# Attention and expert layer: one-block units normed by VectorE before the transposition, moved steps, idle TensorE products

## The chip, the cores and the metric

The kernel runs on one core of a Trainium2 chip. A core has five engines with queues of their own: TensorE (PE: matrix products and transpositions, into PSUM; PEld is its weight load), VectorE (DVE), ScalarE (ACT), GpSimd (POOL) and SyncE (SP, which issues most transfers), and 16 DMA engines shared by all queues. TensorE's clock is granted at one of two levels, 1.2 or 2.4 GHz; a granted clock of 1.00 is the upper one, 0.50 the lower. The metric is the device time of one execution in microseconds (us), as the median of the runs.

## What is computed

```python
# B, T, M, D, G, H = 2, 1024, 256, 128, 4, 4; all float32
q = rope(einsum('bim,ghmd->bghid', x, w_aq)); k = rope(einsum('bim,gmd->bgid', x, w_ak))
v = einsum('bim,gmd->bgid', x, w_av)
s = einsum('bghid,bgjd->bghij', q * D**-0.25, k * D**-0.25) - 1e30 * (i < j)   # causal
o = einsum('bghij,bgjd->bghid', softmax(s), v)
x = layernorm(x + einsum('bghid,ghdm->bim', o, w_ao))
# router over E = 64 experts in 8 groups: the best 4 groups, then the best 6 experts of a token,
# weights = their sigmoid scores over their sum, times 2.5; at most 48 tokens an expert
y = sum over a token's experts of w * (silu(x @ w_gate) * (x @ w_up)) @ w_down
shared = silu(x @ ws_gate) * (x @ ws_up) @ ws_down
out = layernorm(x + y + shared)
```

## The kernel before

The 2048 tokens are 16 tiles of 128 (`TILES`), 8 to a batch. A unit u (64 of them, `UNITS`) is one tile and one of the 4 key groups: tile u // 4, group u % 4, with 4 query heads. Scores are causal, so the units of a batch's n-th tile need n blocks of 128 keys: `blocks(u)` (line 78) is 1 for units 0 to 3 and 32 to 35, 2 for 4 to 7 and 36 to 39, and 8 for the last tile of a batch.

There are four stages. Projections and rotary embedding come first (to about 150 us), with Q, K and V going through DRAM. Then the units (about 150 to 910). Then the tail of the last tile: its layer norm, router and choice of experts, and the scatter of its token rows into the experts' slots. Last come 32 pairs of experts, whose output rows are added in DRAM by indirect transfers of GpSimd's queue (`sums`, L922), and a final sum and layer norm.

Products at full precision are made in two ways: as fp32, or in three passes of operands that are split into a rounded high part (ScalarE, helper `split`, L938) and the rest (VectorE, helper `low`, L1341, or GpSimd: Q at L886, K of the second batch at L871, output weights at L876, the unit's output at L881).

For one unit the steps are:

- `score`: for each head, TensorE makes the row of scores in `s_ps` (L1193) and adds the causal mask (L1196); VectorE takes its negative maximum (`neg_max`, L1407);
- `exp`: ScalarE makes the exponentials in `probs` and their sum in `row_sum` (L1038);
- `ptrans`: for each block, TensorE transposes the four heads' block (L1203), and ScalarE copies it (`pt`, L1049; or `pt_hi`, L938, and VectorE `pt_lo`, L1341). At a unit's first block VectorE also takes the reciprocal of the sums (L1413) and transposes it in 32x32 squares to `inv_t` (L1414); SP stores it in four transfers to `inverses` (L768), waits until they have landed, and loads it back, the same row for all partitions, to `inv_row` (L772);
- `pv`: TensorE adds the block's product with V in `o_ps` (L1220 as fp32, L1223 as three passes); the output comes out transposed, with the queries along the free dimension, which is why the inverses are wanted as a row;
- `omul`: VectorE waits for `inv_row` and multiplies `o_ps` by it to `ot_raw` (L1425);
- `osplit`, `outproj`, `yadd`: the output's split, its product with the output weights (L1233 as fp32 for the first 12 units, L1242 after), and the sum over groups in `y_sb` (L1437).

Behind a tile's last `yadd` come `norm` (statistics L1441 to L1443, the power on GpSimd L895, the row L1449), `x1t` and `x1lo` (its transposition, L1251, and split), `rtr` (router and shared gate, L1258), `sig`, `shared` (L1463 to L1469), `ht`, `htlo`, `sd`, `zadd` (the shared expert: transposition L1264, product L1274, sum L1527), `pick` 0 to 7 (the choice, L1477 to L1511), `count` (L1268, L1269), `fit`, `place` (L1520 to L1535) and `scat` 0 to 2 (two of the six scatters of a row each, L909).

`schedule()` writes one sequence of steps, `SEQ`, and each engine runs through this same sequence and does its part of every step, in order; semaphores hold it where data isn't there. A head's slot in the sequence is one `score`, the `ptrans`, `pv` of an earlier unit (`late = H + 1` heads behind), one `exp`, and what the tables put there. `BETWEEN` (line 85) places the tile steps: each row has the step, how many tiles back it works, and at which of a tile's 16 heads it stands, one number each for the first, second, third and all further tiles of a batch. `KSPLIT_AT` and `WO_SPLIT_AT` (lines 151, 152) name the units in which a group of the second batch's K and of the output weights is split. `RINGED` steps share three PSUM banks in turn.

The queues in short: TensorE waits in `ptrans` for the unit's four exponentials only; VectorE, in its queue, waits before a unit's reciprocal until the stores of the unit two before have landed, and in `omul` for the load; SP waits in its queue for each landing. In the tail, TensorE waits for each result in turn and then for `attention_left`, which VectorE signals behind the last step (L1538); ScalarE waits until all scatters have landed and loads the slots (`srow`, L1077), for which the first expert's transposition on TensorE (L1287) waits.

## Time and profile before

| | |
|---|---|
| median of 3 runs | 1064.26 us (1063.52 to 1064.9) |
| the profiled execution | 1066.87 us, its span 1065.0 us |
| busy: TensorE, VectorE, ScalarE, GpSimd | 950.3, 710.2, 517.4, 447.2 us |
| mean granted clock | 0.958 |

The profile is of one execution. The page gives its totals, the span in 40 slices of 26.6 us, the chain that ended last (followed back from the last instruction, at each step to what released it) and the costliest groups. The trace behind it answers narrower questions: the instructions of an engine in order, with the idle time before each and what ended it, and the busy time in given stretches. Matmuls overlap, so their durations in a timeline are longer than the time they hold TensorE; the chain gives the latter. An fp32 product is recorded as two instructions. "Issue" is time in which the engine waited for nothing that the profile shows.

### The profile page before, as it was taken

The numbers are of one execution on the slowest core, as the hardware profiler recorded it, in microseconds if no ns is written. First come the engines' busy times: TensorE is split into PE (matmuls) and PEld (weight loads), VectorE is DVE, ScalarE is ACT, GpSimd is POOL, SyncE is SP. The second block draws the span as 40 slices with busy tenths as digits, with TensorE's granted clock in tenths as the row PEclk, the third lists the DMA queues.
The fourth block names the chain that finished last, engine by engine and source line by source line (L and its number), as shares of the span: only waits on it lengthen the run. The fifth ranks groups of instructions, "written<-read, shape, count | busy, mean of one in ns | idle before, by whom it ended". The sixth has DMA issues, their size and how long they took to land.

```text
span 1065.0 us, 17542 instructions
## 1 busy us (share of the span) xinstructions
PE 950.3 (89%) x5448; PEld 733.9 (69%) x5448; DVE 710.2 (67%) x1751; ACT 517.4 (49%) x1139; POOL 447.2 (42%) x390
## 2 busy tenths in 40 slices
PE   8999996979999999999968899999999999478744
PEld 6887875756788878777756667888778777245411
DVE  5989863757767676767657877677777676433326
ACT  4111133545656656565656556556566655134402
POOL 3878872244342414124257534424132231325711
PEclk9999998989999999999999999999999999679968
DMA  8786766422334211211234235321212033999687
GB/s 241 234 265 226 258 227 178 131 94 78 99 88 121 64 50 46 68 40 61 66 103 122 71 95 135 92 75 42 70 42 61 26 108 87 257 260 224 87 280 285
DMA packets 137306, 137.28 MB, mean 129 GB/s; under 512 B 18065, under 2 KB 108805, under 8 KB 137216
## 3 DMA queue, kind: packets, MB, share of 16 engines
q1 hardware_dynamic: 84064, 98.33, 30.0%
q10 hardware_dynamic: 43872, 29.50, 9.3%
...
q14 instruction: 45, 0.37, 0.1%
...
## 4 chain that ended last, share of the span: by engine, by line
PE 68%; DVE 9%; issue 7%; DMA 7%; POOL 3%; SPq 3%; ACT 2%; ACTq 1%; POOLq 0%; DVEq 0%
PE s_ps L1193 16%; PE ring L1203 10%; PE o_ps L1223 10%; PE o_ps L1220 7%; PE s_ps L1172 6%; PE ring L1242 6%; PE ring L1172 5%; DMA sums<-erow,goal_u 3%; SPq L811 2%; PE o_ps L1172 2%; DVE neg_max L1407 2%; PE ring L1233 2%; PE s_ps L1196 1%; POOL slot_rows L909 1%; DMA fsum<-sums 1%
## 5 line engine op out<-in xcount | busy, mean ns | idle before, releaser
L1038 ACT ACTIVATE probs<-s_ps,neg_max 128x128 f32<-128x128 f32 (+7 forms) x256 | 189.4, 740 | 118.8 <-DVE neg_max L1407 110.4
L1193 PE MATMUL s_ps<-kt,qt_hi 128*128 128x512 f32 (+3 forms) x768 | 230.9, 382 | 5.1 <-issue 2.4
L1407 DVE TENSOR_REDUCE neg_max<-s_ps 128x1 f32<-128x128 f32 (+7 forms) x256 | 191.5, 751 | 57.4 <-PE s_ps L1196 55.6
L1203 PE MATMUL ring<-ident,probs 128*128 128x128 f32 x1152 | 177.1, 277 | 19.1 <-ACT probs L1038 10.4
L1193 PEld LDWEIGHTS s_ps<-kt,qt_hi 128*128 128x128 f32 x768 | 137.4, 192 | 50.5 <-issue 29.4
L938 ACT ACTIVATE pt_hi<-ring 128x512 fp32r<-128x512 f32 x168 | 100.1, 596 | 141.1 <-PE ring L1203 138.6
L881 POOL TENSOR_TENSOR ot_lo<-ot_raw,ot_hi 128x512 fp32r<-128x512 f32 x52 | 66.7, 1283 | 240.1 <-ACT ot_hi L938 240.1
L1341 DVE TENSOR_TENSOR pt_lo<-ring,pt_hi 128x512 fp32r<-128x512 f32 x168 | 115.6, 689 | 67.9 <-ACT pt_hi L938 65.4
L1203 PEld LDWEIGHTS ring<-ident,probs 128*128 128x128 f32 x1152 | 128.8, 142 | 43.6 <-issue 24.3
L1223 PE MATMUL o_ps<-pt_hi,v 128*128 128x512 f32 x336 | 144.2, 430 | 0.0
L886 POOL TENSOR_TENSOR qt_lo<-q_raw,qt_hi 128x512 fp32r<-128x512 f32 x64 | 82.3, 1286 | 130.9 <-ACT qt_hi L938 130.5
L1193 PE MATMUL s_ps<-kt,qt_lo 128*128 128x512 f32 (+3 forms) x384 | 133.6, 348 | 0.0
L1220 PE MATMUL o_ps<-pt,v 128*128 128x512 f32 x240 | 125.1, 603 | 0.1
L866 POOL TENSOR_TENSOR prods<-prods 128x512 f32<-128x512 f32 x80 | 108.5, 1383 | 38.3 <-DVE prods L1394 38.0
L909 POOL DMA_INDIRECT slot_rows<-row,slot_u x96 | 94.9, 988 | 57.4 <-DVE slot_u L1535 36.0
L1049 ACT ACTIVATE pt<-ring 128x512 f32<-128x512 f32 x120 | 71.2, 593 | 50.0 <-PE ring L1203 49.8
L1425 DVE TENSOR_TENSOR ot_raw<-o_ps,inv_row 128x512 f32<-128x512 f32 x64 | 44.1, 689 | 58.7 <-PE o_ps L1223 33.3
L1193 PEld LDWEIGHTS s_ps<-kt,qt_lo 128*128 128x128 f32 x384 | 73.3, 191 | 8.2
L1223 PEld LDWEIGHTS o_ps<-pt_hi,v 128*128 128x128 f32 x336 | 63.8, 190 | 7.6 <-DVE pt_lo L1341 0.5
L1242 PE MATMUL ring<-wo,ot_hi 128*128 128x256 f32 x416 | 63.3, 295 | 5.9 <-ACT ot_hi L938 4.5
L1223 PE MATMUL o_ps<-pt_lo,v 128*128 128x512 f32 x168 | 66.3, 394 | 0.0
L922 POOL DMA_INDIRECT sums<-erow,goal_u x32 | 46.7, 1458 | 35.2 <-DVE dve_cell L1557 14.1
...
## 6 DMA issues: line engine op xcount, KB each, us to landing
...
q_raw<-qk_rows ACTq DMA_DIRECT2D x128, 128.0 KB, 2.9
...
```

The lines of the kernel that those rows point to most:

```text
L866: pool.tensor_tensor(pair[:, z, 0, :], pair[:, z, 0, :], pair[:, z, 1, :], op).then_inc(rot_ready, 1)
L909: pool.indirect_dma_start(slot_rows[:, :], bass.IndirectOffsetOnAxis(ap=slot_u[:, i % 2, k:k + 1], axis=0), row[:, i % 2, :], None, bounds ...
L938: return act.activation(hi, raw, ACT.Copy)
L1038: act.activation(probs[:, u % 2, h, 0:blocks(u) * P], s_ps[:, n % 2, score_cols(n)], ACT.Exp, bias=neg_max[:, n % 8:n % 8 + 1], accum_out= ...
L1172: ins = pe.matmul(bank(s), *sides, start=(turn == 0), stop=(turn == len(PROJ_PASSES) - 1))
L1193: pe.matmul(s_ps[:, n % 2, c + a:c + e], q[qp], k[kp][:, a:e], start=(qp == kp == 0), stop=(qp == 1 and not last))
L1203: ins = pe.transpose(bank(s)[:, h * P:(h + 1) * P], probs[:, u % 2, h, j * P:(j + 1) * P], ident[:, :])
L1220: ins = pe.matmul(o_ps[:, :], v_sb[i // NT][:, g, j, :], pt[:, n % PTB, :], start=first, stop=last)
L1223: ins = pe.matmul(o_ps[:, :], v[:, g, vp, j - VF, :], (pt_hi, pt_lo)[pp][:, n % PTB, :], start=False, stop=(last and vp == 1))
L1242: ins = pe.matmul(bank(s)[:, 0:M], (ot_hi, ot_lo)[op][:, h * P:(h + 1) * P], wo[:, g, wp, h, :], start=(op == wp == h == 0), stop=(op == 1 ...
L1341: return dve.tensor_tensor(lo, raw, hi.bitcast(F32), ALU.subtract)
L1407: dve.tensor_reduce(neg_max[:, n % 8:n % 8 + 1], s_ps[:, n % 2, score_cols(n)], AX_X, ALU.max, negate=True).then_inc(max_ready, 1)
```

## The change

1. Units of one block (`normed_first`: 0 to 3 and 32 to 35) no longer send their inverses through DRAM. At `ptrans`, behind the reciprocal, VectorE multiplies `probs` of all four heads by it in place (128x512, fp32) and signals `inv_ready`, for which TensorE's transposition now waits too. `omul` is a copy for them. SP's counts of these transfers go over the other units only (`normed_later`).
2. In `BETWEEN`, steps of a batch's second and third tile stand one head later: `ht`, `htlo`, `sd`, `zadd` of the tile two back, the first scatter in the third tile, `x1t` in both, `x1lo`, `rtr`, `sig` in the second, and in the third the next tile's `pick` 0, `ht`, `htlo`.
3. K's last group for the second batch is split one unit earlier (33 in place of 34), and its low part is made by VectorE and not by GpSimd. The output weights are split one head earlier in units 8 to 11.
4. TensorE makes fp32 products of the identity with itself, 128x128x128, into PSUM that nobody reads (`keep_at_work`): 8 ahead of the last tile's `x1t`, 10 ahead of its `ht`, 16 ahead of its `count`, 26 behind `attention_left`, then a wait until the last scatters have landed, then 8.

```diff
--- before.py
+++ after.py
@@ -84,13 +84,13 @@
 
 BETWEEN = [
     (("pick", 0), -2, (None, 0, 0, None)),
-    (("ht",), -2, (None, 1, 0, None)),
-    (("htlo",), -2, (None, 2, 1, None)),
+    (("ht",), -2, (None, 2, 1, None)),
+    (("htlo",), -2, (None, 3, 2, None)),
     (("pick", 1), -2, (None, 1, 1, None)),
     (("pick", 2), -2, (None, 2, 1, None)),
-    (("sd",), -2, (None, 3, 2, None)),
+    (("sd",), -2, (None, 4, 3, None)),
     (("pick", 3), -2, (None, 2, 2, None)),
-    (("zadd",), -2, (None, 4, 2, None)),
+    (("zadd",), -2, (None, 5, 3, None)),
     (("pick", 4), -2, (None, 3, 2, None)),
     (("pick", 5), -2, (None, 3, 2, None)),
     (("pick", 6), -2, (1, 4, 3, 0)),
@@ -98,21 +98,21 @@
     (("count",), -2, (2, 6, 5, 2)),
     (("fit",), -2, (2, 6, 5, 2)),
     (("place",), -2, (4, 7, 6, 4)),
-    (("scat", 0), -2, (5, 8, 7, 5)),
+    (("scat", 0), -2, (5, 8, 8, 5)),
     (("osplit",), -1, (6, 6, 6, 6)),
     (("outproj",), -1, (7, 7, 7, 7)),
     (("yadd",), -1, (8, 8, 7, 7)),
     (("scat", 1), -2, (9, 10, 9, 6)),
     (("norm",), -1, (9, 9, 8, 8)),
-    (("x1t",), -1, (11, 11, 9, 9)),
-    (("x1lo",), -1, (12, 12, 10, 9)),
+    (("x1t",), -1, (11, 12, 10, 9)),
+    (("x1lo",), -1, (12, 13, 10, 9)),
     (("scat", 2), -2, (13, 13, 13, 7)),
-    (("rtr",), -1, (13, 13, 11, 10)),
-    (("sig",), -1, (14, 14, 12, 10)),
+    (("rtr",), -1, (13, 14, 11, 10)),
+    (("sig",), -1, (14, 15, 12, 10)),
     (("shared",), -1, (15, 15, 12, 10)),
-    (("pick", 0), -1, (None, None, 13, 11)),
-    (("ht",), -1, (None, None, 13, 12)),
-    (("htlo",), -1, (None, None, 14, 12)),
+    (("pick", 0), -1, (None, None, 14, 11)),
+    (("ht",), -1, (None, None, 14, 12)),
+    (("htlo",), -1, (None, None, 15, 12)),
     (("pick", 1), -1, (None, None, 14, 13)),
     (("sd",), -1, (None, None, 15, 13)),
     (("zadd",), -1, (None, None, 15, 13)),
@@ -148,7 +148,7 @@
     return seq
 
 
-KSPLIT_AT = [NT * G - G + n for n in (1, 2, 3, 6)]
+KSPLIT_AT = [NT * G - G + n for n in (1, 2, 3, 5)]
 WO_SPLIT_AT = [8, 9, 10, 11]
 FIRST_ROUNDED = 3 * G
 WO_AT = [("exp", 1, 1), ("exp", 1, 3), ("exp", 2, 0), ("exp", 2, 2)]
@@ -156,6 +156,19 @@
 V_LOAD_AT = [(NT - 1) * G + n for n in (1, 2, 7, 8)]
 VSPLIT_AT = [NT * G + n for n in (2, 3, 5, 6)]
 BLANK_AT = [(c, name, 0, 1) for c in range(CHUNKS) for name in (0, 2)]
+
+
+NORMED_FIRST = 1
+
+
+def normed_first(u):
+
+    return blocks(u) <= NORMED_FIRST
+
+
+def normed_later(u):
+
+    return sum(not normed_first(n) for n in range(u))
 
 
 def schedule():
@@ -239,7 +252,7 @@
             drain(i * G)
         if h == 1 and u in KSPLIT_AT:
             seq.append(("ksplit", 1, KSPLIT_AT.index(u)))
-        if h == 3 and u in WO_SPLIT_AT:
+        if h == 2 and u in WO_SPLIT_AT:
             seq.append(("wosplit", WO_SPLIT_AT.index(u)))
         misc(i, n % (G * H))
     p = TILES - 1
@@ -760,14 +773,14 @@
                         load_x(TILES + s[1] + XB)
                     for i in range(s[1] + 1 if s[1] else 0, min(s[1] + 2, TILES)):
                         blank_sums(i)
-                if s[0] == "ptrans" and s[2] == 0:
-                    u = s[1]
+                if s[0] == "ptrans" and s[2] == 0 and not normed_first(s[1]):
+                    u, n = s[1], normed_later(s[1])
                     sp.wait_ge(inv_ready, u + 1)
-                    used(sp, inv_loaded[u % 2], 16 * (u // 2))
+                    used(sp, inv_loaded[u % 2], 16 * (n // 2))
                     for a in range(P // 32):
                         sp.dma_start(inverses[u % 2, :].rearrange("(h a q) -> a h q", h=H, q=32)[a, :, :],
                                      inv_t[32 * a:32 * a + H, u % 2, :]).then_inc(inv_stored, 16)
-                    sp.wait_ge(inv_stored, 64 * (u + 1))
+                    sp.wait_ge(inv_stored, 64 * (n + 1))
                     used(sp, o_ready, u - 1)
                     sp.dma_start(inv_row[:, u % 2, :],
                                  inverses[u % 2:u % 2 + 1, :].to_broadcast([P, P * H])
@@ -865,7 +878,7 @@
                     for z, op in enumerate((ALU.subtract, ALU.add)):
                         pool.tensor_tensor(pair[:, z, 0, :], pair[:, z, 0, :], pair[:, z, 1, :], op
                                            ).then_inc(rot_ready, 1)
-                if s[0] == "ksplit" and s[1] == 1:
+                if s[0] == "ksplit" and s[1] == 1 and s[2] < G - 1:
                     b, g = s[1:]
                     pool.wait_ge(k_hi_ready, G * b + g + 1)
                     pool.tensor_tensor(kt_lo[:, g, :], k_source(b, g), kt_hi[:, g, :].bitcast(F32),
@@ -1133,6 +1146,11 @@
                 elif r >= PRE_BANKS:
                     pe.wait_ge(ring_read[r - RING], PRE_TURNS[r - RING])
 
+            def keep_at_work(n):
+
+                for _ in range(n):
+                    pe.matmul(s_ps[:, 0, 0:P], ident[:, :], ident[:, :], start=True, stop=True)
+
             pe.wait_ge(ident_ready, 1)
             for s in SEQ:
                 kind = s[0]
@@ -1199,6 +1217,8 @@
                 if kind == "ptrans":
                     u, j = s[1:]
                     pe.wait_ge(probs_ready, H * (u + 1))
+                    if normed_first(u):
+                        pe.wait_ge(inv_ready, u + 1)
                     for h in range(H):
                         ins = pe.transpose(bank(s)[:, h * P:(h + 1) * P], probs[:, u % 2, h, j * P:(j + 1) * P],
                                            ident[:, :])
@@ -1245,6 +1265,8 @@
                     ins.then_inc(attn_ready, 1)
                 if kind == "x1t":
                     i = s[1]
+                    if i == TILES - 1:
+                        keep_at_work(8)
                     pe.wait_ge(x1_ready, i + 1)
                     xc = row[:, i % 2, 0:M].rearrange("t (p c) -> t c p", c=MC)
                     for c in range(MC):
@@ -1260,10 +1282,14 @@
                                             start=(c == 0 and xp == wp == 0), stop=(c == MC - 1 and xp == 1))
                     ins.then_inc(rtr_ready, 1)
                 if kind == "ht":
+                    if s[1] == TILES - 1:
+                        keep_at_work(10)
                     read(pe, ("rtr", s[1]))
                     pe.transpose(bank(s)[0:F, 0:P], hid[:, :], ident[:, :]).then_inc(ht_ready, 1)
                 if kind == "count":
 
+                    if s[1] == TILES - 1:
+                        keep_at_work(16)
                     pe.wait_ge(chose_ready, s[1] + 1)
                     pe.matmul(bank(s)[:, 0:E], before_bf[:, :], chose[:, :], start=True, stop=False)
                     pe.matmul(bank(s)[:, 0:E], ones_bf[:, :], taken[:, :], start=False, stop=True
@@ -1277,6 +1303,9 @@
 
 
             pe.wait_ge(attention_left, 1)
+            keep_at_work(26)
+            pe.wait_ge(scattered[(TILES - 1) % 2], 8 * K * TILES)
+            keep_at_work(8)
 
             def slots_t(n):
                 if n in CHUNK_AT:
@@ -1396,6 +1425,10 @@
                     g = s[2]
                     dve.wait_ge(k_hi_ready, g + 1)
                     low(kt_lo[:, g, :], k_source(0, g), kt_hi[:, g, :]).then_inc(k_ready, 1)
+                if s == ("ksplit", 1, G - 1):
+                    dve.wait_ge(k_hi_ready, B * G)
+                    dve.wait_ge(k_ready, B * G - 1)
+                    low(kt_lo[:, G - 1, :], k_source(1, G - 1), kt_hi[:, G - 1, :]).then_inc(k_ready, 1)
                 if kind == "projv" and VF <= s[1] < NT:
                     j = s[1] - VF
                     dve.wait_ge(v_hi_ready, j + 1)
@@ -1409,9 +1442,14 @@
                 if kind == "ptrans" and s[2] == 0:
                     u = s[1]
                     dve.wait_ge(probs_ready, H * (u + 1))
-                    used(dve, inv_stored, 64 * (u - 1))
+                    used(dve, inv_stored, 64 * (normed_later(u) - 1))
                     after(dve.reciprocal(inv_sum[:, u % 2, 0:H], row_sum[:, u % 2, :]))
-                    dve.transpose(inv_t[:, u % 2, :], inv_sum[:, u % 2, :]).then_inc(inv_ready, 1)
+                    if normed_first(u):
+                        raw = probs[:, u % 2, :, 0:blocks(u) * P]
+                        dve.tensor_tensor(raw, raw, each(inv_sum[:, u % 2, 0:H], blocks(u) * P), ALU.mult
+                                          ).then_inc(inv_ready, 1)
+                    else:
+                        dve.transpose(inv_t[:, u % 2, :], inv_sum[:, u % 2, :]).then_inc(inv_ready, 1)
                 if kind == "ptrans" and s[2] >= VF:
                     n = PT_AT[s[1:]]
                     dve.wait_ge(p_hi_ready, PS_AT[s[1:]] + 1)
@@ -1419,10 +1457,14 @@
                 if kind == "omul":
                     u = s[1]
                     i, g = divmod(u, G)
-                    dve.wait_ge(inv_loaded[u % 2], 16 * (u // 2 + 1))
                     dve.wait_ge(pv_done, PT_AT[(u, blocks(u) - 1)] + 1)
                     used(dve, attn_ready, u - 1)
-                    dve.tensor_tensor(ot_raw[:, u % 2, :], o_ps[:, :], inv_row[:, u % 2, :], ALU.mult).then_inc(o_ready, 1)
+                    if normed_first(u):
+                        dve.tensor_copy(ot_raw[:, u % 2, :], o_ps[:, :]).then_inc(o_ready, 1)
+                    else:
+                        dve.wait_ge(inv_loaded[u % 2], 16 * (normed_later(u) // 2 + 1))
+                        dve.tensor_tensor(ot_raw[:, u % 2, :], o_ps[:, :], inv_row[:, u % 2, :], ALU.mult
+                                          ).then_inc(o_ready, 1)
                 if kind == "yadd":
                     u, s = s[1], ("outproj", s[1])
                     i, g = divmod(u, G)
```

## Rows read from the trace of the kernel before

**Rows 1.** The page: clock by slice, and chain that ended last, by engine.
```profile
PEclk9999998989999999999999999999999999679968
...
PE 68%; DVE 9%; issue 7%; DMA 7%; POOL 3%; SPq 3%; ACT 2%; ACTq 1%; POOLq 0%; DVEq 0%
```

**Rows 2.** Stretches (us): busy time (instructions) of PE, PEld, DVE, ACT, POOL; granted clock; DMA share.
```profile
164.70:173.20 8.50, 0.00 (x0) 0.00 (x0) 2.22 (x8) 0.92 (x5) 0.00 (x0) 0.75 0.70 198
...
173.20:179.30 6.10, 6.07 (x23) 4.69 (x24) 2.28 (x6) 3.56 (x11) 1.26 (x1) 0.51 0.39 125
...
228.00:234.00 6.00, 5.97 (x22) 5.04 (x23) 3.03 (x8) 2.20 (x7) 1.91 (x2) 0.51 0.37 126
```

**Rows 3.** Chain that ended last, in order of time (start, us, what).
```profile
160.23 5.83 DMA inverses<-inv_t
...
166.07 5.26 DMA inv_row<-inverses
...
179.84 1.73 PE ring L1233 x8
...
234.78 0.71 PE ring L1258 x6
```

**Rows 4.** TensorE's timeline: start, us, instruction [idle before, what ended it].
```profile
173.23 1.09 PE L1203 MATMUL ring<-ident,probs 128*128 128x128 f32 x4 [8.56 <-ACT probs L1038]
...
201.88 0.29 PE L1264 MATMUL ring<-ident,hid 128*96 128x128 f32 x1 [1.58 <-DVE hid L1469]
...
228.03 0.67 PE L1251 MATMUL ring<-ident,row 128*128 128x128 f32 x2 [4.19 <-DVE row L1449]
...
240.49 0.28 PE L1264 MATMUL ring<-ident,hid 128*96 128x128 f32 x1 [2.44 <-DVE hid L1469]
...
546.90 0.41 PE L1193 MATMUL s_ps<-kt,qt_hi 128*128 128x128 f32 x2 [2.44 <-issue]
...
558.67 0.36 PE L1274 MATMUL ring<-wsd_hi,ht_hi 96*128 96x256 f32 x1 [2.41 <-DVE ht_lo L1341]
...
618.87 0.28 PE L1264 MATMUL ring<-ident,hid 128*96 128x128 f32 x1 [1.69 <-DVE hid L1469]
```

**Rows 5.** Groups of VectorE by form: busy us, mean ns.
```profile
L1604 DVE TENSOR_TENSOR fsum<-fsum 128x512 f32<-128x512 f32 x20 | 13.8, 690 | 31.2 <-DMA fsum<-sums 30.8
...
L1341 DVE TENSOR_TENSOR kt<-kt 128x1024 fp32r<-128x1024 f32 x4 | 4.9, 1229 | 0.0
```

**Rows 6.** Timelines of VectorE and GpSimd, one collision.
```profile
586.70 2.26 DVE L1477 TENSOR_TENSOR biased<-sig,bias_sb 128x64 f32<-128x64 f32 x1
...
587.58 1.30 POOL L886 TENSOR_TENSOR qt_lo<-q_raw,qt_hi 128x512 fp32r<-128x512 f32 x1
```

**Rows 7.** GpSimd's timeline behind the second tile.
```profile
220.93 2.37 POOL L876 TENSOR_TENSOR wo<-wo_raw,wo 128x1024 fp32r<-128x1024 f32 x1 [7.02 <-ACT wo L938]
...
225.90 0.59 POOL L895 TENSOR_TENSOR rstd<-var_eps,minus_half 128x1 f32<-128x1 f32 x1
```

**Rows 8.** ScalarE's and VectorE's timelines at unit 32.
```profile
534.79 0.60 ACT L1049 ACTIVATE pt<-ring 128x512 f32<-128x512 f32 x1 [0.49 <-PE ring L1203]
...
535.83 0.17 DVE L1413 RECIPROCAL inv_sum<-row_sum 128x4 f32<-128x4 f32 x1
...
536.64 0.69 DVE L1425 TENSOR_TENSOR ot_raw<-o_ps,inv_row 128x512 f32<-128x512 f32 x1 [0.22 <-issue]
```

**Rows 9.** Chain that ended last, in the tail.
```profile
917.94 1.64 PE ring L1258 x6
...
920.80 0.24 DVE biased L1477
...
923.47 0.19 DVE chose L1502
...
941.88 1.49 PE s_ps L1297 x8
...
947.32 0.81 PE s_ps L1297 x8
```

## The prediction

> **What bounds the kernel now.** I read the page first. The chain that ended last lies on TensorE for 68% of the span, with VectorE, DMA and "issue" far behind, and the granted clock is full in nearly all slices except around the seventh, the ninth and tenth, and the last five [rows 1]. So the middle of the kernel is TensorE work at full speed that nothing in the change touches, and a gain has to come from places where TensorE stands still or runs at 1.2 GHz. I then cut the span into stretches and read TensorE's timeline for what ends each pause. There are three such places: the start of each batch (units 0 to 11 and 32 to 43, where score rows are 1 to 3 blocks long), and the tail behind the last unit.
>
> The largest pause is at the start: TensorE does nothing at all from 164.70 to 173.20 and works the next 6.1 us at half clock [rows 2]. Its row says "waits for ScalarE's exponentials" [rows 4], but the chain shows the root: four stores of the inverse sums, 5.83 us to land, then their broadcast load, 5.26 us [rows 3]. VectorE stands in its queue behind the first (the reciprocal of unit 2 waits until unit 0's stores have landed) and then behind the second (the product with unit 0's inverses), so the row maxima of unit 3 come late, then its exponentials, then TensorE.
>
> **A. Units 0 to 3 normed before the transposition.** For these the change removes four stores, one load, and both waits of VectorE. It adds one in-place product of 128x512, both inputs in SBUF, for which the nearest row is the addition of two such tiles, 690 ns [rows 5]. The 32x32 transposition goes (about 0.2 us, not counted), and the output product becomes a copy of the same 128x512 out of PSUM; I take that as no cheaper. The new wait is TensorE's: the transposition of a unit now waits for reciprocal and product, 0.17 [rows 8] + 0.69 = 0.9 us behind the last exponential. Behind it on TensorE are the next scores, and behind those the next row maxima. Written out unit by unit, each of units 0 to 3 gets some 0.7 us longer (0.9 less what the Q split's wait hides), so the fourth transposition comes at 167.8, an estimate, in place of 173.23 [rows 4]; the clock then had no idle stretch to fall in, so the 6.0 us of unit 4 that ran at half clock become about 3.6 us, where ScalarE's exponentials set the pace. Unit 4's transposition comes at 171.4 in place of 179.2: **gain 7.8 us**. From there to 190 TensorE has no pause before, so the shift stays. What is late next: the output weights, loaded by GpSimd's queue just before the pause and used by the first output product, which moves from 179.84 [rows 3] to 172; and the Q tiles. The DMA engines are still at 0.70 in the pause [rows 2]. Bounds: 5 us (both late by 1.5 us, and each product held up) to 9 us.
>
> **B. Steps of tiles 1 and 2 set apart, output-weight split one head earlier.** Three pauses: 1.58, 4.19 and 2.44 us [rows 4]. The 4.19 one is a queue on GpSimd: it splits output weights for 2.37 us, issues two row scatters, and only then raises the variance to -0.5 (at 225.90) [rows 7], for which VectorE's normalisation and TensorE's transposition of x1 wait. The scatter moves one head back, behind the power, and the transposition one head back too, so I expect this pause to go; the same holds for 1.58 and 2.44, whose transposition of the hidden tile gets one more head (1.2 us or more of TensorE work) ahead of it. That is 8.2 us at most; I count 6.0, as the split, one head earlier, now holds GpSimd while VectorE ranks the experts (a collision, below). The 6 us from 228 on ran at half clock [rows 2]; without the pause they take some 3.5. I count 2.0. **Gain 8.0 us**, bounds 3 and 11.
>
> **C. Units 32 to 35, and the last K split.** The split of K's last group goes from GpSimd (2.34 us and a pause of 2.44 us on TensorE [rows 4]) to VectorE, one unit earlier: 1.23 us [rows 5]. Gain 2.4. The hidden tile's step moves: 2.41 us [rows 4], of which I count 1.4; 1.2 for a half-clock spell at 548. Against that: here no wait on the inverses is to be seen, so the normed product brings nothing and costs its wait. Unit 32's transposition was through by 534.8, but VectorE came to its reciprocal at 535.83 only, behind the ranking of tile 6 [rows 8]. TensorE will now stand from before 534.8 until 536.9 (535.83 + 0.9, and a hand-over), then VectorE waits for ScalarE's K copy and splits K before it evacuates unit 31, so that this comes at about 540 in place of 536.64 [rows 8]: -3.5. The other three units cost 0.5 each. **Net 0**, bounds -4 and +3.
>
> **D. Tiles 8 to 10.** The same pauses as in B without the weight split, 1.69 us the largest [rows 4], about 5 us in all. VectorE is nearly full here. **Gain 2.0**, bounds 0 and 4.
>
> **E. The tail.** An idle product is an fp32 128x128x128; eight fp32 instructions of 256 columns, four products, took 1.73 us [rows 3], so 0.22 us each at full clock and 0.43 at half. The first eight start at half clock and end some 0.6 us after the row they should have ended before: -0.6. Then the router's six products, 1.64 us here and 0.71 at full clock [rows 9, 3], and two transpositions: +1.3. The sixteen ahead of the count have from about 919 to 923.5, when the choice is written [rows 9], and need 3.5 us at full clock. The ten and the 26 lie under VectorE's and the scatters' time. If the clock is then high when the first experts start, their group of eight takes 0.81 in place of 1.49 us [rows 9], and the first output row comes 2.4 us earlier; since the scatters behind it stand under weight loads until 975, I count 1.3 of it. **Gain 2.0**, bounds -2 and 4.
>
> **A new wait.** Where pauses are this close, closing one shows another; for the pauses of 0.3 to 0.7 us that appear at new places I take off **2.0**.
>
> **Sum.** 7.8 + 8.0 + 0 + 2.0 + 2.0 - 2.0 = 17.8 us. The profiled execution took 1066.87 us (span 1065.0), so it would come to 1049.1; the median of the runs is 2.6 us lower, 1064.26, and the forecast for it is 1064.26 - 17.8 = **1046.5 us**.
>
> **A rule that speaks against it.** VectorE's addition of the bias, two inputs in SBUF, took 2.26 us beside GpSimd's splits (one ended at 587.6, the next started at once) and 0.24 us where GpSimd was quiet [rows 6, 9]. The Trainium skill says the same (SBUF — State Buffer, "SBUF: two separate sides"): VectorE and GpSimd share a port pair, and whichever of a GpSimd operation and a two-input VectorE operation starts first has it to its end. So the new product can be held up by a Q split of 1.30 us [rows 6]. In my unit-by-unit order it starts 0.3 us before the Q split, and the split waits instead; so the sum holds nothing for it.
>
> **The rivals.**
> (1) The early gain is eaten by loads: Q tiles or output weights are late, so TensorE meets a DMA wait in place of the inverses'. The DMA engines' share of 0.70 in the pause [rows 2] speaks for it, that nothing waited for these loads before says little. A gives 3 in place of 7.8, and half of the clock's part of B goes: 1052.5.
> (2) The moved steps only shift the pauses, because VectorE is the limit there: B gives 3, D 0: 1053.5.
> (3) Slower: each of the eight normed products finds GpSimd at a Q split and waits for it. Then a transposition is late by 0.9 + 1.3 = 2.2 us in eight units, 17.6 us; that is 10.8 over the 0.7 x 4 + 0.5 x 8 counted, and with pauses like the 4.19 us one, behind which the clock fell, it falls again (A and B lose 5, E 2) and C's queue doubles (-3.5): 17.8 - 10.8 - 7 - 3.5 = -3.5, so 1067.8. It decides as soon as the product starts behind the split in most units.
> (4) The change does not do what it says, the clock stays at half through the tail and the idle products run over: E is -2: 1050.5. This lies in the forecast's own range.
>
> **Chances.** Forecast with (4): 0.60; (1) 0.14; (2) 0.17; (3) 0.06; rest 0.03 for a loss or standstill by something not seen. The forecast's range is 1040 to 1051; taking in (1) and (2), and the upper bounds of A and B on the other side, 1039 to 1056. A difference of under 0.2%, 2.1 us, can't be told from none: faster 0.92, same 0.03, slower 0.05.
>
> **What would show it.** Right: no pause of over 2 us on TensorE between 150 and 250, and no half-clock stretch behind 164; unit 4's transposition near 171; a TensorE wait of 0.7 to 1 us on VectorE's new product in units 0 to 3; the x1 transposition of tile 1 without a pause; a TensorE pause of 2 to 3 us near unit 32's transposition; the clock at full for the last router and for the first experts. Wrong: pauses ended by DMA behind unit 3; VectorE products of over 1.5 us at the new line; the sixteen idle products still running when the choice is written.

## The result, and the profile after

The changed kernel took 1072.46 us (median of 20 runs, 1062.71 to 1077.33), the kernel before 1062.99 us beside it (20 runs, 1056.99 to 1066.07): ratio 1.0084, 95% interval 1.0066 to 1.0102. It is 0.8% slower, 8.9 us by the ratio, where 1046.5 us and a gain were forecast, with a range of 1040 to 1051. The profiled execution took 1068.99 us, so the two profiles are only 2.1 us apart where the medians are 9.5 apart. Both profiles are off their medians, in opposite directions: that of before is long at its start, that of after short behind unit 63 (table below). Stretches are therefore read over all profiles, not from these two alone.

Clock by slice and the chain that ended last, on the page of the changed kernel (answers to [rows 1]):
```profile
PEclk9999988999999999999969999999999999999968
...
PE 72%; DVE 10%; issue 5%; DMA 5%; SPq 2%; ACT 2%; POOL 1%; ACTq 1%; POOLq 0%; DVEq 0%
```
The dip of the ninth slice is gone, the one at the sixth and seventh (units 0 to 5) is wider; a new one, deeper than both, stands in slice 21, at units 33 to 36, and the tail keeps its clock better.

TensorE's pauses in the changed kernel (start, us, instruction, in brackets the idle time before it and what ended it; answers to [rows 4]):
```profile
152.46 0.66 PE L1223 MATMUL ring<-ident,probs 128*128 128x128 f32 x4 [1.63 <-DVE probs L1449]
157.93 1.09 PE L1223 MATMUL ring<-ident,probs 128*128 128x128 f32 x4 [1.82 <-DVE probs L1449]
163.83 1.08 PE L1223 MATMUL ring<-ident,probs 128*128 128x128 f32 x4 [1.83 <-DVE probs L1449]
...
198.31 1.99 PE L1253 MATMUL ring<-wo_raw,ot_raw 128*128 128x256 f32 x8 [1.02 <-DVE hid L1511]
...
231.16 3.55 PE L1253 MATMUL ring<-wo_raw,ot_raw 128*128 128x256 f32 x8 [1.81 <-DVE hid L1511]
...
240.25 0.36 PE L1300 MATMUL ring<-wsd_hi,ht_hi 96*128 96x256 f32 x1 [2.70 <-DVE ht_lo L1370]
...
530.08 0.63 PE L1223 MATMUL ring<-ident,probs 128*128 128x128 f32 x4 [2.55 <-DVE probs L1449]
535.50 2.05 PE L1262 MATMUL ring<-wo,ot_hi 128*128 128x256 f32 x8 [2.65 <-ACT ot_hi L951]
541.61 0.69 PE L1223 MATMUL ring<-ident,probs 128*128 128x128 f32 x4 [2.27 <-DVE probs L1449]
547.39 1.09 PE L1223 MATMUL ring<-ident,probs 128*128 128x128 f32 x4 [1.78 <-DVE probs L1449]
557.73 1.08 PE L1223 MATMUL ring<-ident,probs 128*128 128x128 f32 x4 [4.09 <-DVE probs L1449]
```
The pause of 8.56 us has become one in each unit, ended by the new product (L1449). In the L1223 rows the second column is the same four transpositions at two speeds: about 0.63 us at full clock, 1.09 at half. Two of the three early ones shown run at half. The clock fell behind the first of these pauses: it was granted at 1.00 from 144.40 to 152.46 and at 0.54 from there to the next transposition.

Why a unit takes so long, in VectorE's timeline for unit 2 of the changed kernel:
```profile
160.49 0.29 DVE L1440 TENSOR_REDUCE neg_max<-s_ps 128x1 f32<-128x128 f32 x1 [0.48 <-PE s_ps L1214]
161.27 0.29 DVE L1440 TENSOR_REDUCE neg_max<-s_ps 128x1 f32<-128x128 f32 x1 [0.48 <-PE s_ps L1214]
162.04 0.29 DVE L1440 TENSOR_REDUCE neg_max<-s_ps 128x1 f32<-128x128 f32 x1 [0.48 <-PE s_ps L1214]
162.25 0.17 DVE L1446 RECIPROCAL inv_sum<-row_sum 128x4 f32<-128x4 f32 x1
162.45 1.24 DVE L1449 TENSOR_TENSOR probs<-probs,inv_sum 128x512 f32<-128x512 f32 x1
```
The maxima come every 0.77 us, each behind TensorE's score (in e8, the filled kernel below, TensorE needs 0.41 for one). The reciprocal stands behind the one at 162.04, which belongs to head 1 of the *next* unit. The product then takes 1.24 us, not 0.69. TensorE's transposition waits for all of it, and the next scores wait behind that. Not every product is held up like this one. The other seven took 1.04, 1.23 and 0.69 us in units 0, 1 and 3, and 0.69, 0.69, 1.19 and 0.69 us in units 32 to 35. Three of the eight (units 1, 2 and 34) began while GpSimd was at a Q split; the one of unit 0 began while it was at another operation, a product of the rotary embedding. The ones of units 34 and 35:
```profile
546.06 1.19 DVE L1449 TENSOR_TENSOR probs<-probs,inv_sum 128x512 f32<-128x512 f32 x1
556.89 0.69 DVE L1449 TENSOR_TENSOR probs<-probs,inv_sum 128x512 f32<-128x512 f32 x1
```

Stretches of the two kernels (us from:to, length; busy time and instructions of PE, PEld, DVE, ACT, POOL; granted clock; DMA share and GB/s). In the kernel before, units 0 to 4, and 32 to 45:
```profile
147.32:178.23 30.91, 20.87 (x120) 17.19 (x120) 11.23 (x34) 12.44 (x48) 12.87 (x12) 0.80 0.62 191
518.68:644.07 125.39, 106.71 (x674) 82.91 (x673) 90.36 (x271) 72.52 (x192) 67.60 (x57) 0.99 0.33 94
```
The same two in the changed kernel, with the worst part of the first between them:
```profile
144.40:174.10 29.70, 23.00 (x120) 19.36 (x120) 14.38 (x34) 13.12 (x47) 13.84 (x12) 0.71 0.58 176
150.00:168.00 18.00, 12.71 (x69) 11.21 (x68) 8.12 (x21) 8.83 (x32) 9.21 (x9) 0.62 0.73 212
511.96:650.16 138.20, 114.40 (x674) 88.98 (x674) 92.65 (x272) 72.33 (x192) 65.79 (x56) 0.91 0.27 77
```
Units 32 to 45 take 12.8 us more. TensorE's instructions are the same 674 in number, but it is busy 7.7 us longer with them (clock 0.91 in place of 0.99) and stands 5.1 us longer. The early stretch has lost its long pause and yet is hardly shorter.

All 16 experiments and the changed kernel, as ratio to the kernel before with its 95% interval, and the length of four stretches of each profile, in us. A stretch goes from the first score of head 0 of one unit (the product of its causal mask, L1214 after) to that of the other; the last one goes to the end of the span.

| kernel | ratio | units 0 to 5 | 5 to 20 | 32 to 46 | 63 to end |
|---|---|---|---|---|---|
| before | | 30.9 | 158.4 | 125.4 | 188.5 |
| changed | 1.0084 (1.0066–1.0102) | 29.7 | 155.8 | 138.2 | 184.7 |
| e1 no unit normed | 0.9990 (0.9966–1.0015) | 29.5 | 156.9 | 128.1 | 187.2 |
| e2 norm alone | 1.0113 (1.0079–1.0148) | 32.1 | 157.5 | 138.4 | 187.6 |
| e3 units 0–3 only | 0.9986 (0.9961–1.0011) | 30.7 | 156.5 | 127.8 | 186.8 |
| e4 no idle products | 1.0099 (1.0069–1.0130) | 30.5 | 156.4 | 135.5 | 189.3 |
| e5 old steps | 1.0062 (1.0025–1.0098) | 32.3 | 157.0 | 134.3 | 187.1 |
| e8 filled | 1.0024 (0.9997–1.0052) | 22.5 | 157.2 | 134.9 | 186.2 |
| e9 by head | 1.0138 (1.0105–1.0170) | 35.1 | 157.0 | 138.6 | 189.6 |
| e10 early | 1.0034 (1.0008–1.0060) | 24.6 | 155.9 | 134.7 | 185.5 |
| e11 idle products alone | 0.9995 (0.9969–1.0022) | 29.6 | 156.8 | 125.8 | 190.1 |
| e12 first four | 0.9891 (0.9851–0.9932) | 21.8 | 155.2 | 125.2 | 188.4 |
| e13 + K on VectorE | 0.9915 (0.9888–0.9942) | 21.8 | 155.4 | 123.3 | 189.4 |
| e14 filled and early | 0.9984 (0.9961–1.0008) | 23.7 | 156.0 | 134.3 | 189.8 |
| e15 steps alone | 1.0018 (0.9997–1.0039) | 29.2 | 157.1 | 128.8 | 187.5 |
| e16 steps filled | 0.9970 (0.9952–0.9989) | 31.4 | 157.4 | 124.9 | 185.5 |
| e17 gap filled | 0.9951 (0.9927–0.9975) | 26.5 | 155.8 | 125.8 | 187.1 |
| e18 + one pause filled | 0.9899 (0.9865–0.9934) | 21.9 | 155.5 | 125.0 | 188.6 |

Each ratio is against the kernel before as it ran beside that experiment; one execution of e12 (1374.95 us) and one of the kernel before (1234.96 us) ran in a slower state and are left out. Each stretch is from one profile. Kernels that differ in nothing inside a stretch show how far one profile can be off: units 32 to 46 took 138.2 us in the changed kernel and 135.5 in e4, 123.3 in e13 and 125.0 in e18, 128.1 in e1 and 127.8 in e3; units 0 to 5 took 30.9 in the kernel before and 29.6 in e11. Where a stretch and the ratios differ, the ratios over all runs decide.

### The profile page after: what moved, and what is told of

The parts are those of the page before. It is cut to its first block, busy times and chain, and to the rows that moved or that the text cites. A ratio compares the mean times of both kernels' runs of the same rounds, so it can differ in the third digit from the quotient of the medians.

```text
span 1067.2 us, 17751 instructions
## 1 busy us (share of the span) xinstructions
PE 972.3 (91%) x5584; PEld 755.1 (71%) x5584; DVE 717.1 (67%) x1752; ACT 516.8 (48%) x1139; POOL 446.6 (42%) x389
## 4 chain that ended last, share of the span: by engine, by line
PE 72%; DVE 10%; issue 5%; DMA 5%; SPq 2%; ACT 2%; POOL 1%; ACTq 1%; POOLq 0%; DVEq 0%
PE s_ps L1211 17%; PE ring L1223 11%; PE o_ps L1243 10%; PE o_ps L1240 8%; PE ring L1262 6%; PE s_ps L1190 6%; PE ring L1190 5%; DMA sums<-erow,goal_u 3%; SPq L824 2%; PE ring L1253 2%; DVE neg_max L1440 2%; PE o_ps L1190 2%; PE s_ps L1214 1%; DMA fsum<-sums 1%; PE ring L1280 1%
## 5 line engine op out<-in xcount | busy, mean ns | idle before, releaser
L1051 ACT ACTIVATE probs<-s_ps,neg_max 128x128 f32<-128x128 f32 (+7 forms) x256 | 189.3, 740 | 114.4 <-DVE neg_max L1440 105.2
L1211 PE MATMUL s_ps<-kt,qt_hi 128*128 128x512 f32 (+3 forms) x768 | 237.3, 391 | 1.5 <-DVE prods L1423 1.5
L1223 PE MATMUL ring<-ident,probs 128*128 128x128 f32 x1152 | 178.0, 278 | 24.9 <-DVE probs L1449 17.4
L1211 PEld LDWEIGHTS s_ps<-kt,qt_hi 128*128 128x128 f32 x768 | 141.3, 198 | 50.9 <-issue 31.6
L1223 PEld LDWEIGHTS ring<-ident,probs 128*128 128x128 f32 x1152 | 129.3, 143 | 49.7 <-issue 33.3
L1240 PE MATMUL o_ps<-pt,v 128*128 128x512 f32 x240 | 128.2, 617 | 0.2
L922 POOL DMA_INDIRECT slot_rows<-row,slot_u x96 | 95.6, 996 | 57.2 <-issue 32.3
L1466 DVE TENSOR_TENSOR ot_raw<-o_ps,inv_row 128x512 f32<-128x512 f32 x56 | 38.5, 688 | 42.0 <-PE o_ps L1243 37.4
L1262 PEld LDWEIGHTS ring<-wo,ot_hi 128*128 128x128 f32 x416 | 54.3, 192 | 15.3 <-issue 7.3
```

The costliest lines, as they stand in the source:

```text
L922: pool.indirect_dma_start(slot_rows[:, :], bass.IndirectOffsetOnAxis(ap=slot_u[:, i % 2, k:k + 1], axis=0), row[:, i % 2, :], None, bounds ...
L1051: act.activation(probs[:, u % 2, h, 0:blocks(u) * P], s_ps[:, n % 2, score_cols(n)], ACT.Exp, bias=neg_max[:, n % 8:n % 8 + 1], accum_out= ...
L1211: pe.matmul(s_ps[:, n % 2, c + a:c + e], q[qp], k[kp][:, a:e], start=(qp == kp == 0), stop=(qp == 1 and not last))
L1223: ins = pe.transpose(bank(s)[:, h * P:(h + 1) * P], probs[:, u % 2, h, j * P:(j + 1) * P], ident[:, :])
L1240: ins = pe.matmul(o_ps[:, :], v_sb[i // NT][:, g, j, :], pt[:, n % PTB, :], start=first, stop=last)
L1262: ins = pe.matmul(bank(s)[:, 0:M], (ot_hi, ot_lo)[op][:, h * P:(h + 1) * P], wo[:, g, wp, h, :], start=(op == wp == h == 0), stop=(op == 1 ...
```

## The experiments

### Which part of the change costs the time

e1, no unit normed:
```diff
-NORMED_FIRST = 1
+NORMED_FIRST = 0
```


> The changed kernel with no unit normed ahead of its transposition; moved steps, the K split on VectorE and the idle products stay. Theory N (the normed product is what made the change slower: in the profiles, units 32 to 45 lose 12.9 us, and TensorE's pauses there, 2.55, 2.65, 2.27, 1.78 and 4.09 us, are mostly ended by the normed product or what is queued behind it): the loss of 12.9 goes and the 8.5 us pause at unit 2 comes back, so about 8 to 12 us less than the kernel before, ratio 0.989 to 0.993. Theory S (the moved steps and the K split on VectorE caused the loss of 32 to 45): it stays slower than before, 1.003 to 1.010.


e3, `return u < 4` in `normed_first`:


> The changed kernel with units 0 to 3 alone normed; units 32 to 35 go by the stored inverses again. Theory N: the loss of units 32 to 45 goes, the early part stays at its gain of 6.7 us up to unit 20, the tail gives its 4: 9 to 13 us less than before, ratio 0.988 to 0.992, within 3 us of the kernel without any normed unit. Theory S: the loss in units 32 to 45 stays, ratio 1.003 to 1.010.


e2, the kernel before with the norm for the eight units and nothing else:


> The kernel before with units 0 to 3 and 32 to 35 normed ahead of the transposition, and nothing else of the change. Theory N: slower than before by 9 to 14 us (1.008 to 1.013), with units 32 to 45 losing some 12 us and units 0 to 3 gaining next to nothing. Theory S: within 3 us of the kernel before, as the product costs only its own 0.7 us or so each, and unit 2's pause is saved. My forecast's own terms for it would have been a gain of about 3 (7.8 less 3.5 and 1.5).


Measured: 0.9990, 0.9986 and 1.0113. The norm alone makes the kernel slower by 12 us (8 to 16), at least as much as the whole change's 9 (7 to 11), and the loss of units 32 to 46 goes with units 32 to 35 (138.2 to 128.1 or 127.8). The ratios say so by themselves: e3 differs from the changed kernel in units 32 to 35 alone and is 0.0098 below it, 10.4 us (7 to 14). Theory N holds for the place and the size of the loss. Its further claim, that 8 to 12 us of gain would then come out, fails: without the norm the rest of the change is worth about 1 us (e1's interval goes from 3.6 us faster to 1.6 slower). Nor do units 0 to 3 gain by their norm: e3 has it and e1 does not, and they are 0.4 us apart. Something is left in units 32 to 46 all the same, as the stretch of e1 shows (TensorE's busy time is the number behind the length):
```profile
513.81:641.87 128.06, 110.05 (x675) 85.96 (x674) 90.80 (x272) 72.19 (x192) 66.21 (x56) 0.96 0.33 92
```
That is 2.7 us over the kernel before, all of it in busy time (110.05 against 106.71) at a clock of 0.96: it is taken up below.

e4, no idle products in the tail (`for _ in range(0 * n)` in `keep_at_work`), and e11, the kernel before with them alone:


> The changed kernel without the idle products in the tail. If they give the 4 us that the profiles show behind unit 63 (clock at full for the last router and the first experts), it is 3 to 5 us slower than the changed kernel: ratio to the kernel before 1.011 to 1.014. If the sixteen products that overrun the choice eat the clock's gain, it is the same as the changed kernel or 1 us faster, 1.007 to 1.009.

> The kernel before with the idle products of the tail alone; no other part of the change. My forecast's term for them was 2.0 us, bounds -2 and 4. In six profiles with them the stretch behind unit 63 was 1.8 us shorter on the mean than in the kernel before, in two without them 0.1 shorter. Expected if that holds: 1 to 3 us less, ratio 0.997 to 0.999. If the sixteen that overrun the choice eat it up: 0.999 to 1.001.


Measured 1.0099 and 0.9995, against 1.0084 and 1: a gain of 1.6 and of 0.5 us, neither distinct from none. The 1.8 us that e11 was to confirm came from too few profiles. The stretch behind unit 63 took 187.6 us on the mean of 13 profiles with the products and 188.0 on that of 5 without, and scatters by 5 us. In the changed kernel the clock is high there (the router's six products take 0.95 us in place of 1.64), but the sixteen overrun. Two pieces of the chain that ended last in the changed kernel (start, us, what), the router and then the sixteen:
```profile
923.41 0.95 PE ring L1280 x6
924.36 5.20 PE s_ps L1152 x32
```
And the step of VectorE's timeline, same kernel, that they were to end ahead of, the choice:
```profile
928.28 0.20 DVE L1544 TENSOR_SCALAR chose<-left 128x64 bf16<-128x64 f32 x1
```
The choice is there at 928.48, the sixteen products (32 instructions) end at 929.56: 1.1 us late, partly at half clock. So these take back at least a part of what the clock gives; no run has the other idle products without the sixteen.

e5, old places of the steps and of the output weights' split, all else as changed; e15, the kernel before with only the new places:


> The changed kernel with the old places of the steps between the heads and of the output weight split; normed units, K split on VectorE and idle products stay. My forecast counted 10 us for them (8.0 at tiles 1 and 2, 2.0 at tiles 8 to 10) and 1.4 of the hidden tile's: then this kernel is 8 to 11 us slower than the changed one, ratio 1.016 to 1.019. If the steps only move the pauses (in the profiles the five pauses of 0.6 to 2.7 us between 198 and 241 add up to 7.1 us where three made 8.2 before): within 3 us of the changed kernel, ratio 1.006 to 1.011.

> The kernel before with the moved steps and the output weight split one head earlier, and nothing else of the change. My forecast's terms for it were 8.0 (tiles 1 and 2), 2.0 (tiles 8 to 10) and 1.4: 11 us less, ratio 0.990. If the steps only move the pauses, 0 to 2 us less, 0.998 to 1.000. If, as the kernel without normed units suggests (units 32 to 46 took 128.1 us in place of 125.4, with 3.3 us more of TensorE's work time and no more pause), the new pauses of over 3 us let the clock fall: 0 to 4 us more, 1.000 to 1.004.


Measured 1.0062 and 1.0018. Against the changed kernel the old places are 2.3 us faster and against the kernel before the new ones 1.9 us slower, neither clear of noise; a gain of 10 us is excluded. The pauses only moved. Of the three between 200 and 241 in the kernel before, 1.58, 4.19 and 2.44 us [rows 4], the 4.19 us one is indeed gone. In the changed kernel there are 1.02 and 0.61 us near 200 instead, then 0.92, 1.81 and 2.70 us between 224 and 241, 7.1 us in place of 8.2; in e1, e8, e10 and e15 the last of them is 4.3 us. VectorE is late with `hid` and `ht_lo` once the other step no longer holds TensorE.

### Why the normed product costs so much

Three edits to the changed kernel, each on one suspected cause. e8 puts TensorE to work ahead of its wait (theory G, clock):
```diff
+FILL = 6
...
                 if kind == "ptrans":
                     u, j = s[1:]
+                    if normed_first(u):
+                        for _ in range(FILL):
+                            pe.matmul(bank(s)[:, 0:P], ident[:, :], ident[:, :], start=True, stop=True)
                     pe.wait_ge(probs_ready, H * (u + 1))
```


> The changed kernel with six more idle products ahead of the first transposition of each normed unit, written into the PSUM bank that the transposition then overwrites. Theory G (the 1.4 to 1.8 us that TensorE stands for the normed product in each unit keep its clock at half, and the half clock lengthens the scores of the loop, 0.77 in place of 0.46 us a head): with TensorE at work the clock stays at full, a unit takes 4 to 4.5 us in place of 5.9 to 6.8, units 0 to 3 gain 4 us or more and 32 to 35 about as much, ratio to the kernel before 0.999 to 1.003. Theory P (the length of the product beside GpSimd's Q split, 1.04 to 1.24 in place of 0.69 us, and its place in the queue set the pace, the clock does not): no gain, ratio 1.007 to 1.011.


e9 writes the product as four of one input each (theory P, port):
```diff
-                        dve.tensor_tensor(raw, raw, each(inv_sum[:, u % 2, 0:H], blocks(u) * P), ALU.mult
-                                          ).then_inc(inv_ready, 1)
+                        for h in range(H):
+                            ins = dve.tensor_scalar(raw[:, h, :], raw[:, h, :], inv_sum[:, u % 2, h:h + 1], None,
+                                                    ALU.mult)
+                        ins.then_inc(inv_ready, 1)
```


> The changed kernel with the product written as four products of 128x128 by one column each, a form with one tile as input in place of two. Theory P (two tiles read from SBUF by VectorE collide with GpSimd's split): the four together take the same 0.7 to 0.9 us beside a split as alone, the split is no longer stretched to 1.8 us, the pauses get 0.4 us shorter, 2 to 4 us less than the changed kernel, ratio 1.005 to 1.007. Theory G alone: the product's length is a third of the pause at most, ratio 1.007 to 1.010.


e10 moves reciprocal and product ahead of the row maximum of the next unit's head 1 (theory Q, queue). Beside the lines shown, the block that takes the row maximum (`if kind == "score"`) moves behind this one:
```diff
-                if kind == "ptrans" and s[2] == 0:
-                    u = s[1]
+                if (kind == "ptrans" and s[2] == 0 and not normed_first(s[1])
+                        or kind == "score" and s[2] == 1 and s[1] >= 1 and normed_first(s[1] - 1)):
+                    u = s[1] if kind == "ptrans" else s[1] - 1
```


> The changed kernel with reciprocal and product one step earlier in VectorE's order, ahead of the row maximum of head 1 of the next unit (in the changed kernel they stand behind it, and it waits for its score on TensorE). Theory Q (the place in VectorE's queue is what makes TensorE wait): the product starts 0.7 to 0.9 us earlier in each of the eight units, pauses of 1.4 to 1.8 us become 0.6 to 0.9 us; 4 to 8 us less than the changed kernel, ratio 1.001 to 1.005. Theory G or P without Q: the maximum now waits for the product in its turn, so the score loop is as long as before, ratio 1.007 to 1.010.


e8 came to 1.0024, 6.4 us less than the changed kernel, and e10 to 1.0034, 5.3 us less (each give or take 3.5). So the clock and the place in the queue both count. By the table most of that lies in units 0 to 5, 7.2 and 5.1 us; in units 32 to 46 the two are at 134.9 and 134.7 us, under the changed kernel's 138.2 but hardly under e4's 135.5. Units 0 to 4 in e8:
```profile
146.19:168.67 22.48, 22.20 (x168) 19.83 (x168) 13.07 (x34) 12.39 (x46) 14.58 (x12) 1.00 0.76 227
```
48 instructions more than in the changed kernel and 7.2 us less, at a clock of 1.00 in place of 0.71. TensorE is busy for all but 0.3 us. The faster scores also let the product start before GpSimd's split in units 1 to 3, so that it took 0.69 us (timeline of e8, unit 1):
```profile
157.00 0.69 DVE L1453 TENSOR_TENSOR probs<-probs,inv_sum 128x512 f32<-128x512 f32 x1
157.17 1.65 POOL L900 TENSOR_TENSOR qt_lo<-q_raw,qt_hi 128x512 fp32r<-128x512 f32 x1
```
In e10 the pauses of units 1 and 2 fell from 1.82 and 1.83 to 0.51 us each, at a clock of 0.79 over the stretch. The shorter pauses alone did not bring the clock back. Behind the 1.64 us of unit 0 it fell, and the transpositions of units 1 and 2 still ran at half (TensorE's timeline in e10):
```profile
157.37 0.63 PE L1223 MATMUL ring<-ident,probs 128*128 128x128 f32 x4 [1.64 <-DVE probs L1444]
160.96 1.09 PE L1223 MATMUL ring<-ident,probs 128*128 128x128 f32 x4 [0.51 <-DVE probs L1444]
165.54 1.09 PE L1223 MATMUL ring<-ident,probs 128*128 128x128 f32 x4 [0.51 <-DVE probs L1444]
```

e9 went the other way, 1.0138. Its four small products took 0.87 us where GpSimd was quiet and up to 2.18 beside GpSimd's work (VectorE's timeline in e9, units 0, 1 and 32):
```profile
153.90 2.18 DVE L1450 TENSOR_SCALAR probs<-probs,inv_sum 128x128 f32<-128x128 f32 x4
...
160.20 1.50 DVE L1450 TENSOR_SCALAR probs<-probs,inv_sum 128x128 f32<-128x128 f32 x4
...
536.92 0.87 DVE L1450 TENSOR_SCALAR probs<-probs,inv_sum 128x128 f32<-128x128 f32 x4
```
So one input in place of two is no way around the collision here. P's assumption of the form is refuted; that the collision costs is not. How much it costs can be bounded: over the eight products of the changed kernel, what each took beyond 0.69 us adds up to 1.9 us (2.9 in the profiles of e2 and e4), of a loss of 9. In unit 1 of the changed kernel the split ran from 155.98 to 157.24 and the product, begun at 156.55, ended 0.54 us after it; with the order turned, in e8 above, it is the split that grows, from 1.26 to 1.65. The Trainium skill has the rule (SBUF — State Buffer, "SBUF: two separate sides": the one that starts first has the shared ports for the whole instruction, the other is blocked). By it the product would take the rest of the split, 0.69, and its own 0.69, 1.38 us; the trace has 1.23, so it agrees but for 0.15 us.

e14, both cures (six idle products and the earlier place) in all eight units:


> The changed kernel, all eight units normed, with both cures at once: product one step earlier and six idle products ahead of each normed transposition. Each alone gave 5 to 6 us. If they act on the same pause (the clock for one, its length for the other), together they give 7 to 10 of the 9 us lost, ratio 0.998 to 1.001; if the idle products now take longer than the pause they fill, 1.001 to 1.004. Above 0.999 it is behind the version that norms units 0 to 3 alone, since units 32 to 35 wait for no inverses.


Measured 0.9984. The early part keeps its gain, but units 32 to 46 are still at 134.3 us, 6.2 over e1. There the product replaces no wait. VectorE comes to it late from other steps, and 24 idle products have to be paid: against e1, TensorE is busy 5.6 us longer (115.65 against 110.05) and stands 0.6 longer. No cure made the norm pay in units 32 to 35.

### The clock by itself

e17, the kernel before with 32 idle products ahead of unit 3's transposition, in the 8.56 us pause:
```diff
+FILLED = {("ptrans", 3, 0): 32}
...
+                for _ in range(FILLED.get(s, 0)):
+                    pe.matmul(bank(s)[:, 0:P], ident[:, :], ident[:, :], start=True, stop=True)
```


> The kernel before, its pause of 8.6 us ahead of unit 3's transposition filled with 32 idle products (7.0 us at full clock), and nothing else. It measures the clock's part of that pause by itself: unit 4's scores and the transpositions behind the pause ran 6 us at half clock in the kernel before. If the clock is kept by any work of TensorE, units 0 to 5 take 27 us in place of 29.6, ratio 0.997 to 0.999; if it falls all the same, 29.6 us, 0.999 to 1.001.


Units 0 to 4 of e17, the same stretch as above:
```profile
145.74:172.28 26.54, 24.14 (x184) 21.56 (x184) 10.27 (x32) 11.84 (x45) 12.90 (x12) 1.00 0.70 215
```
0.9951, 5.2 us gained without touching the wait for the inverses, and the clock is 1.00 throughout. The interval is 2.6 to 7.8 us. In the profile the stretch is 3.0 us shorter than in e11, whose instructions up to there are the same but for the filling, and units 5 to 20 are 0.9 shorter.

e16, e1 with 12 and 11 idle products in the two 3.3 us pauses that the new step places leave in units 32 to 37 (`FILLED = {("outproj", 31): 12, ("sd", 7): 11}`, with the same loop):


> The kernel without normed units, its two pauses of 3.3 us in units 32 to 37 (ahead of an output product, ahead of the shared experts' product of tile 7) filled with 12 and 11 idle products. If half clock behind these pauses is the 3 us that the moved steps cost there, units 32 to 46 go from 128.1 to about 125 us and no slice there is under full clock; ratio 0.995 to 0.998. If the pauses themselves are the cost, nothing moves, 128 us, 0.998 to 1.001.


Units 32 to 45 of e16:
```profile
517.61:642.48 124.87, 111.99 (x721) 87.87 (x720) 90.70 (x272) 72.24 (x192) 66.34 (x56) 0.99 0.33 94
```
Clock 0.99 in place of 0.96, 124.9 in place of 128.1 us, ratio 0.9970 in place of 0.9990. So the 3 us that the moved steps cost there are the clock behind longer pauses, as expected; this rests on the stretch, as the two ratios' intervals overlap. The idle products themselves took 0.24 us each (24 instructions, 2.90 us, ahead of the output product).

### A version that beats both

e12: old steps, old K split, idle products of the tail, units 0 to 3 normed with the earlier place and four idle products each. e13: the same with K's last group on VectorE.


> Old steps, old K split, the idle products of the tail, and units 0 to 3 normed with both cures at once: reciprocal and product ahead of head 1's row maximum, and four idle products in front of each normed transposition. By the trace of the filled kernel, which gained 8.4 us between units 0 and 5, and by 1.8 us in the tail: 7 to 10 us less than the kernel before, ratio 0.990 to 0.993. If the two cures do not add and idle products now stand in the transposition's way (four are 0.9 us at full clock, the pause left was 0.5 at half): 3 to 6 us less, 0.994 to 0.997.

> The same as the kernel of the first four units, but K's last group of batch 2 is split by VectorE one unit earlier, as in the changed kernel. My forecast counted a gain of 2.4 us for it: then 2 to 3 us less than without it. If VectorE is what TensorE waits for in units 32 to 37, its 1.2 us there are added in part: 0 to 2 us more than without it.


Units 0 to 4 of e12:
```profile
147.92:169.76 21.84, 20.64 (x152) 18.06 (x152) 13.28 (x34) 12.37 (x46) 13.92 (x12) 1.00 0.79 238
```
0.9891 and 0.9915: 9 to 12 us less than the kernel before and, with e18 below, the fastest measured. The early stretch is 7.8 us shorter than in e11, the same number as term A's. Some 3 us of it e17 has too, by filling the old pause and without any norm. The K split takes 1.9 us off units 32 to 46 between these two profiles, but e18, with the same split, is at 125.0, 0.2 under e12; the forecast of 2.4 is neither confirmed nor excluded, and the ratios can't tell the two kernels apart.

e18: e13 with 16 idle products ahead of the transposition of tile 1's rows:


> The version with units 0 to 3 normed and K's last split on VectorE, with 16 idle products in the pause of 4.2 us ahead of the transposition of tile 1's rows. The clock stood at half for some 5 us behind that pause: 1 to 3 us less than without them, units 5 to 20 in 153.5 us in place of 155.4, ratio 0.987 to 0.991. If the pause has its own length from VectorE and GpSimd and the clock falls later all the same: as without them, 0.991.


0.9899: 1.7 us under e13 and 0.9 over e12, neither a difference that can be told. The pause of 4.20 us shrank to 0.53 and TensorE reached the hidden tile's step some 1.6 us earlier; there the wait for `hid` was as long as before (2.44 against 2.43), the clock fell behind that pause instead (0.70 from 225 to 230), and the stretch stayed at 155.5 us. My expectation of 153.5 us for this stretch failed; the ratio lies in the span that I expected, and the gain of 1 to 3 us is neither shown nor excluded by it.

## Why the prediction was wrong

**A, forecast +7.8, measured about -1.** The mean of units 0 to 5 is 30.1 us over the five profiles that norm nothing and fill nothing there, e16 among them, and 31.1 over the five with the changed kernel's norm. The ratios of e3 and e1, with and without this norm, are 0.4 us apart. Three statements of the step failed. (1) "0.17 + 0.69 = 0.9 us behind the last exponential": the reciprocal also stands behind the maximum of the next unit's head 1. (2) "the product starts 0.3 us before the Q split": in units 1 and 2 of the kernel as built it started 0.57 us behind it and took 1.23 and 1.24 us. (3) "the clock then had no idle stretch to fall in": the pauses of 1.6 to 1.8 us in every unit were enough here, and the mean clock from 150 to 168 was 0.62. I had written waits of 0.7 to 0.9 us a unit into the sum and never asked what they do to the clock. With TensorE kept at work and the product one step earlier, two edits that the forecast did not have, the early stretch does come out 7.8 us shorter (e12); that it is the very number forecast is partly luck.

**B and D, forecast +8.0 and +2.0, measured about +1 and -3.** Rival 2's mechanism: the steps only shift pauses. Between units 5 and 20 the means are 157.4 (old places, first batch otherwise uncured: before, e2, e5, e11) and 156.6 us (ten kernels with the new ones). That 0.8 us is not a gain of the places for certain: with the first batch cured, e12, e13, e17 and e18 have the old places and took 155.2 to 155.8 us, e8, e10 and e14 the new ones and 155.9 to 157.2. In units 32 to 46, e15 is 3.0 us longer than e11, e5 3.9 shorter than the changed kernel (1.2 shorter than e4). "I expect this pause to go" came true for the 4.19 us one. The failed step is what follows it, "the same holds for 1.58 and 2.44": in their place stand 1.02, 0.61, 1.81 and 2.70 us (4.3 for the last in e1, e8, e10 and e15). It looked at the step released and not at the next one in VectorE's queue. For D the term also left out the clock behind the new pauses of 3.3 us (e16).

**C, forecast 0, measured about -8 for its own two parts (-5.5 if e4's profile stands for the changed kernel).** The mechanism was as told ("TensorE will now stand from before 534.8"), the K split's 2.4 measured 1.9 in one pair of profiles and 0.2 in another, and the first pause of 2.55 us came as forecast. Mis-sized was "the other three units cost 0.5 each": their pauses are 2.27, 1.78 and 4.09 us. Against e1, with the same steps, the changed kernel is 10.1 us longer there (e4 7.4, the ratios of e3 and the changed kernel 10.4): TensorE stands 5.8 us longer (23.80 against 18.01) and is busy 4.35 us longer (114.40 against 110.05) at lower clock. The last pause lies behind steps of the ranking, one of them 0.94 us beside GpSimd.

**E, forecast +2.0, measured about +0.4, not distinct from none.** The clock is high, as forecast. The overrun of the sixteen was given as a sign of "wrong", and it is there.

**The sum.** Norm early -1.0, steps +0.8 and -3.0, norm late -10.1, K split +1.9, tail +0.4: -11.0 us, against -8.9 (-7.0 to -10.8) by the ratio. Single profiles of the same stretch differ by up to 2.7 us, so this is as close as it gets, and the agreement of the parts is no proof of each.

**The rivals.** Rival 3, given 0.06, is the nearest: normed products held up at GpSimd's split, pauses, and a clock that falls for them; it named 1067.8. Its direction and its clock are right, its main price is not. It charged each of eight products 1.3 us for a split; three of the eight began behind one (four in e2 and e4), and all collisions together lengthened the products by 1.9 us (2.9 there), where it added 10.8 us to the forecast's sum. Nor was its own condition, behind the split in most units, met over the eight. What it had too small is the rest, the clock and VectorE's queue. Its sum also has a slip: it takes off 0.5 us for eight units where the forecast had counted it for three besides unit 32; with four it would have named 1069.8. A reading was off too, without consequence: the clock's second dip is at the ninth slice alone, not at the tenth.

The order that rival 3 has, the product behind the split, was the one that I had ruled out by writing the units out at full clock. That order was itself a result of the clock: with TensorE kept at work (e8) the product does start before the split in units 1 to 3, as it does with the earlier place (e10).

Of the signs of "right", the x1 transposition of tile 1 without a pause, the pause of 2 to 3 us near unit 32 (2.55) and full clock for the first experts came true (their group of eight took 0.81 us), and for the last router nearly (0.95 us in place of 1.64; 0.71 is full clock). Four did not: there was a pause of over 2 us between 150 and 250 (2.70 at 240), half clock behind 164, waits of 1.42 to 1.83 us for the new product in place of 0.7 to 1, and unit 4's transposition came at 175.1, not near 171 (178.0 counted from unit 0's place in the kernel before, which was 2.9 us later). Of the signs of "wrong", the overrun of the sixteen came; no product of this profile took over 1.5 us (one of e4's took 1.69), and no pause behind unit 3 was ended by DMA.

What stays open: how much of the 7 to 10 us in units 32 to 46 is the collision with GpSimd (one product of four, 0.5 us by its duration) and how much each queue on VectorE; no run removed the collision alone. Whether the tail's products bring anything is open: the interval of e11 goes from 3.3 us faster to 2.3 slower.
